# A decoder's per-head attentions on one core: an item's two value products side by side in TensorE's order

## The reference, cut to what matters

```python
# layer 0, self-attention: 16 heads of 16, LoRA projections
scores = einsum('bhqd,bhkd->bhqk', q, k) * SCALE
out = einsum('bhqk,bhkd->bhqd', softmax(scores), v)
# layer 1, self-attention: 16 heads of 16, causal, ALiBi bias
scores = where(causal, scores + bias, NEG)
# layer 1, cross-attention: 32 query heads of 8, 8 key heads
scores = einsum('bkgsd,bktd->bkgst', qh, kh) * scale
out = einsum('bkgst,bktd->bkgsd', softmax(scores), vh)
```

## Time and profile before

| | us |
|---|---|
| median of 3 runs (lowest, highest) | 950.26 (950.02, 950.55) |
| the profiled execution | 950.78 |
| its span in the trace | 948.6 |
| a0, first to last output copy | 63.21 to 118.57 |
| a1, last output copy | 676.35 |
| x1, first to last output copy | 735.67 to 830.39 |

### The profile page before, as it was taken

How to read it: one execution, slowest core, us unless ns; L and a number is a source line. 1 busy time by engine, 2 the same in 40 slices (tenths; PEclk the granted TensorE clock), 3 DMA queues, 4 the chain that set the end, 5 groups by cost and what they waited for, 6 DMA issues and landing times. The chain is left out here.

```text
span 948.6 us, 14084 instructions
## 1 busy us (share of the span) xinstructions
PE 762.5 (80%) x4818; PEld 483.7 (51%) x4818; DVE 592.4 (62%) x1129; ACT 422.8 (45%) x879; POOL 209.7 (22%) x313
## 2 busy tenths in 40 slices
PE   6888968899898998988362458889726999959998
PEld 3544655566666665665221233546512444348787
DVE  5557666564655656655765973456455999673765
ACT  4446732644535436345165334345332666612322
POOL 4312020303203023031303412221031212123441
PEclk9979989999999999999776557999955999987999
DMA  5957413110201201100210008693051111001311
GB/s 127 119 75 129 133 29 88 41 51 16 67 26 42 65 10 58 26 12 23 68 16 23 0 7 99 69 142 89 23 172 54 40 42 38 7 2 23 113 45 45
DMA packets 52356, 53.48 MB, mean 56 GB/s; under 512 B 11296, under 2 KB 41984, under 8 KB 52296
## 3 DMA queue, kind: packets, MB, share of 16 engines
q1 hardware_dynamic: 47772, 51.55, 26.1%
q10 hardware_dynamic: 4524, 1.14, 0.6%
HBM read 29.62 MB, written 5.09 MB: 37 GB/s over the span
## 5 line engine op out<-in xcount | busy, mean ns | idle before, releaser
L536 DVE TENSOR_REDUCE a_nm<-ps 128x2 f32<-128x512 f32 (+1 forms) x112 | 75.6, 688 | 52.0 <-PE ps L836 30.4
L1185 DVE TENSOR_REDUCE x_nm<-ps 128x2 f32<-128x512 f32 x128 | 84.9, 686 | 24.0 <-PE ps L1253 22.1
L679 ACT ACTIVATE a_pt<-ps 128x1024 f32<-128x1024 f32 x64 | 58.0, 916 | 49.1 <-PE ps L887 30.8
L1221 ACT ACTIVATE x_pt<-ps 128x1024 f32<-128x1024 f32 x64 | 62.1, 1021 | 33.1 <-PE ps L1290 33.1
L2007 PE MATMUL ps<-m_xp,m_mp 128*128 128x512 f32 x288 | 74.8, 400 | 1.9 <-DVE m_wr L1735 1.9
L1721 DVE TENSOR_TENSOR m_qcs<-ps,mw_tab 128x512 f32<-128x512 f32 x96 | 61.8, 686 | 22.0 <-PE ps L2007 21.1
L1884 ACT ACTIVATE m_junk<-ps,m_nm 128x256 bf16<-128x256 f32 x128 | 58.7, 486 | 37.0 <-DVE m_nm L1747 37.0
L1707 POOL TENSOR_SCALAR fw<-fw,finv 128x256 f32<-128x256 f32 x24 | 11.7, 486 | 254.8 <-PE ps L2087 254.8
L1253 PE MATMUL ps<-a_ks,a_qs 126*128 126x256 bf16 x256 | 53.3, 294 | 17.6 <-DMA a_ks<-scr_xk 16.1
L2007 PEld LDWEIGHTS ps<-m_xp,m_mp 128*128 128x128 f32 x288 | 52.2, 191 | 14.3 <-issue 4.9
L2816 PE MATMUL ps<-x_xp,x_wp 128*128 128x512 f32 x216 | 55.9, 410 | 0.3 <-DVE x_h3g L2738 0.3
(11 more groups left out here) (271 smaller groups left out, 1714.9 us busy)
## 6 DMA issues: line engine op xcount, KB each, us to landing
a_qs<-a_parts SPq DMA_DIRECT2D x48, 128.0 KB, 6.5
a_ks<-a_parts SPq DMA_DIRECT2D x48, 128.0 KB, 7.4
m_q<-m_qs SPq DMA_DIRECT2D x32, 128.0 KB, 2.2
x_gb<-scr_g SPq DMA_DIRECT2D x8, 512.0 KB, 3.6
fw<-in_f_w SPq DMA_DIRECT2D x12, 256.0 KB, 3.5
scr_xq<-xs_qp SPq DMA_DIRECT2D x12, 256.0 KB
a_qs<-scr_xq SPq DMA_DIRECT2D x32, 96.0 KB, 2.1
mw_wq<-in_m_wq SPq DMA_DIRECT2D x8, 256.0 KB, 2.9
```

Of the source, the lines that this page charges most:

```text
L536: dve.tensor_reduce(dst, src, AX.X, ALU.max, negate=True).then_inc(mx_done.sem, 1)
L679: act.activation(pt[:, n % 2, kt, 0:banks * BANK], c.ps[:, 2 + 2 * kt:2 + 2 * kt + banks, :].rearrange("p b n -> p (b n)"), ACT.Exp, scale ...
L1185: dve.tensor_reduce(dst, src, AX.X, ALU.max, negate=True).then_inc(mx_done.sem, 1)
L1221: act.activation(pt[:, i % 2, kt, 0:banks * BANK], c.ps[:, 2 + 2 * kt:2 + 2 * kt + banks, :].rearrange("p b n -> p (b n)"), ACT.Exp, scale ...
```

## The change

In the step of an item `product(n, 1)` moves up to stand directly behind `product(n, 0)`, ahead of `max_transpose` and of the third unit of scores. `scores_t(n + 1, 1)` moves from the end of the step to the place ahead of the fourth unit. The same edit is made in the loop of `attention_block` and in the body of `attention_stage`. In a1, which has no fourth unit, `scores_t(n + 1, 1)` stays the last of the step. The other engines' lists stay as they are.

```diff
                     scores_t(n + 1, 0)
                     scores(n + LAG, 1)
                     product(n, 0)
+                    product(n, 1)
                     max_transpose(n + TLAG)
                     scores(n + LAG, 2)
-                    product(n, 1)
+                    scores_t(n + 1, 1)
                     if UNITS == 4:
                         scores(n + LAG, 3)
-                    scores_t(n + 1, 1)
...
                         product(it, i, 0)
+                        product(it, i, 1)
                         ahead(max_transpose, it, i + TLAG, last)
                         ahead(scores, it, i + LAG, last, 2)
-                        product(it, i, 1)
+                        ahead(scores_t, it, i + 1, last, 1)
                         if UNITS == 4:
                             ahead(scores, it, i + LAG, last, 3)
-                        ahead(scores_t, it, i + 1, last, 1)
```

## The result

After the change the median is 953.84 us (6 runs, 952.49 to 955.53), the kernel before on the same chip 950.14 us (6 runs, 946.63 to 950.97): ratio 1.0048, 95% interval 1.0028 to 1.0067. The change costs +3.7 us where +8.1 was forecast: slower, as predicted, but by much less, and 0.2 us under 954, the low end of the range. The profiled execution took 954.16 us, its span is 952.0 (before 948.6).

The account below looks back on a forecast made before the run. Waits between TensorE and VectorE were taken to bound a0 and x1, TensorE alone a1. Terms x1 +6.9, a0 +2.5, a1 -1.3 sum to +8.1, giving 958.4 us; range 954 to 962.

Parts of the forecast that it names:

- TensorE's own order is the bound everywhere: Rival, all stages: TensorE's issue order sets every item, -0.2 us an item in x1 and a0, total 942.2; chance 0.09.
- S1 reuses the bank that R3 reads; the weight load ahead of S1 has 0.19 idle: x1 item: the second scores unit waits for the previous fourth reduce, 0.88 us from reduce start to scores.
- same loop; I take x1's +0.25: a0 stage: the same loop of waits as in x1 binds, so each item grows by 0.25 us.
- S0 waits for R2 as well: First scores unit also waits for the third reduce; that end plus 0.19 leads on no later than the fourth reduce.
- 6 x 0.25 = 1.5: a0 stage: six item intervals behind the transfer stall each grow by 0.25 us, +1.5 together.
- The term of x1, +6.9: x1 stage: 28 intervals times 0.24 us give 6.7, plus 0.2 at the end; bounds 5.9 and 7.5.
- the +0.2 for the last M: End of x1: the last `max_transpose` comes 0.46 us later behind the second product, half of it counted.
- the stall ends near 79.4: a0, item 6: the wait for its row of maxima, ending at 78.45 before, would end near 79.4.
- +1.0: a0 stall: SyncE's row of item 5 and the `send_high(3)` sends behind it come later, delaying item 6 by 1.0 us.
- The exponentials are not late: Rival, x1: the second product waits for a late exponential, overdrawn by 0.15 us an item, total 962.6; chance 0.06.
- the clock stays at 1.00: Rival: TensorE's idle of 0.45 us an item lowers its clock to 1.2 GHz; three such items give 966; chance 0.04.
- T1's 0.43 costs nothing now: x1 item before: the second `scores_t`, 0.43 us, lies under the fourth reduce, which holds back the second scores unit anyway.

Follow-up runs that it names:

- T1 back behind S3: The change, with the second `scores_t` again behind the fourth unit of scores in a0 and x1, against the kernel before: 952.87 us, ratio 1.0030.
- a0 alone: Only the a0 call of `attention_block` takes the new order, against the kernel before: 949.48 us, ratio 1.0001.
- x1 alone: Only the loop body of `attention_stage` takes the new order, against the kernel before: 953.84 us, ratio 1.0042.
- a1 alone: Only the a1 call of `attention_block` takes the new order, against the kernel before: 948.55 us, ratio 0.9987.

## Why the prediction was right and where it was wrong

**Right: TensorE's own time in the new order.** A0 to M was put at 0.92 and took 0.88; A0 to S2 at 1.07 and took 1.04 in x1 and 1.09 in a0. The Trainium skill (TensorEngine Tiling (Array Packing), Key Properties) says that changing the tiling mode drains TensorE. The runs show what the borders between products and other matmuls cost: an item of a1, which TensorE alone sets, is 0.24 shorter with two such borders fewer. That it is a drain no run shows by itself.

**Right that x1's loop binds, and by luck its length: the path is O's and not S1's.** From R3 to A0 the prediction counted 0.88 + 0.37 = 1.25 by way of S1, and it is 1.25 before (776.29 to 777.54) and after (778.31 to 779.56). But the path is R3, O, A0: 0.60 + 0.41 + 0.24; the way through S1 needs only about 1.07 (below). The two lengths agree because both were read off the same two events. The same chain closes to 3.18 before: 1.25 + 0.46 + 0.15 + 0.32 + 0.57 + 0.43. So in x1 VectorE's loop did bind ahead of the change, if barely: the items beside the loop's ends are 3.13 apart, where A0 follows S1 by 0.31 in TensorE's own order. From there on all that A1 adds ahead of S2 is paid. The rival "TensorE's own order is the bound everywhere" falls with that: x1 got 4.8 slower.

**The step that failed: "S1 reuses the bank that R3 reads; the weight load ahead of S1 has 0.19 idle", priced as R3 to S1 0.88 and carried to a0 ("same loop; I take x1's +0.25").** The idle was the weight load's at 777.03. The matmul S1 at 777.17 was due then anyway, by TensorE's own order: T0 at 776.74 and 0.43 more. 0.88 was the spacing of two events with slack between them, not the length of a dependency. After the change R3 ends at 778.99 and the matmul starts at 779.06, so R3 to S1 is at most 0.75, and 0.13 of the 0.88 was slack. In x1 this did no harm, since O's path makes up the 1.25. In a0 it did, since O's end leads to A0 sooner there. The timeline of a0 after:

```profile
93.08 1.07 PE L901 MATMUL ps<-a_pt,a_vs 128*32 128x256 f32 x16
...
94.18 0.39 PE L823 MATMUL ps<-a_ks,a_qs 96*128 96x256 bf16 x2
...
94.61 1.35 DVE L536 TENSOR_REDUCE a_nm<-ps 128x2 f32<-128x512 f32 x2 [0.46 <-PE ps L823]
...
95.87 0.41 DVE L544 TENSOR_SCALAR xnT<-ps 128x256 f32<-128x256 f32 x1
...
96.02 0.39 PE L823 MATMUL ps<-a_ks,a_qs 96*128 96x256 bf16 x2
...
96.34 0.85 PE L901 MATMUL ps<-a_pt,a_vs 128*32 128x256 f32 x12
```

O ends at 96.28 and A0 starts 0.06 later; R3 (95.28) to S1 is 0.74 and S1 to A0 0.32. By both ways R3 to A0 is about 1.06, not 1.25. With 1.10 to S2, 0.43 to R2 and 0.67 to R3 that makes 3.26. But a third way gives the same sum here: S0 waits for R2, and TensorE's own order leads on to S1 and A0. T1 back behind S3 tells them apart, since it brings R3 forward. The timeline of an a0 item of that kernel:

```profile
91.41 1.07 PE L901 MATMUL ps<-a_pt,a_vs 128*32 128x256 f32 x16
...
92.51 0.61 PE L823 MATMUL ps<-a_ks,a_qs 96*128 96x256 bf16 x4
...
92.94 1.29 DVE L536 TENSOR_REDUCE a_nm<-ps 128x2 f32<-128x512 f32 x2 [0.51 <-PE ps L823]
...
93.69 0.39 PE L823 MATMUL ps<-a_ks,a_qs 96*128 96x256 bf16 x2
...
94.14 0.41 DVE L544 TENSOR_SCALAR xnT<-ps 128x256 f32<-128x256 f32 x1
...
94.36 0.38 PE L823 MATMUL ps<-a_ks,a_qs 96*128 96x256 bf16 x2
```

R3 (0.61 after R2, at 93.55) ends 0.13 ahead of S1 (94.36), and O ends 0.12 ahead of the next A0 (94.67): neither is waited for, and still the item is 3.26. The loop is R2 to S0 0.75, S1 0.67, A0 0.31, S2 1.10, R2 0.43 = 3.26. With O moved away a0 has 3.26 as well. The prediction had this wait too ("S0 waits for R2 as well"), with the same 0.19 in it, and so with the same slack.

A0 and A1 of an a0 item before:

```profile
70.20 0.64 PE L901 MATMUL ps<-a_pt,a_vs 128*32 128x256 f32 x8
...
71.19 0.64 PE L901 MATMUL ps<-a_pt,a_vs 128*32 128x256 f32 x8
```

With A1 to S3 0.57 and S3 to R3 0.43 the loop through R3 was 1.06 + 0.99 + 0.57 + 0.43 = 3.05, 0.15 short of TensorE's own 3.20. The change used up that slack and 0.06 more. The term of a0's six items, "6 x 0.25 = 1.5", would be 6 x 0.06 = 0.4; a0 alone measures 0.6 (19.63 for the six intervals, before 19.05), since the last of them is 3.26 where it was 3.07.

**The term of x1, +6.9, was mis-sized: +4.8.** 0.04 of each item because A1 and M took 0.88 and not 0.92, and 0.02 because R2 to R3 is 0.66 and not 0.68: 3.38 in place of 3.43, where 3.41 was the forecast of 3.17 + 0.24. And not all items pay that: in the last body and beside the loop's ends they were 3.13 apart before and are 3.27 after, so +0.14. The output copies of x1 after (they answer to the earlier trace rows) give the sum:

```profile
735.20 0.41 DVE L1190 TENSOR_SCALAR x_av<-ps 128x256 f32 x1
...
825.53 0.41 DVE L1190 TENSOR_SCALAR x_av<-ps 128x256 f32<-128x256 f32 x1
```

90.33 for 27 intervals, before 85.52: +0.18 an item on average, 4.8. The last four copies take 9.18, before 9.20: the +0.2 for the last M is nothing.

**a1: right, and a little more than forecast.** The timeline of a1 after (it answers to the earlier trace rows), a product pair, M and S2:

```profile
654.75 0.86 PE L901 MATMUL ps<-a_pt,a_vs 128*32 128x256 f32 x16
...
655.42 0.28 PE L853 MATMUL ps<-identb,a_nms 128*8 128x128 bf16 x2
...
655.63 0.39 PE L831 MATMUL ps<-a_ks,a_qs 102*128 102x256 bf16 x2
```

A0 to M is 0.67, forecast 0.46 + 0.25 = 0.71. The item is 3.20, 0.24 under 3.44 and not 0.20. Over six intervals that is -1.4: from A0 of item 6 to A0 of item 12 it takes 18.50 after, and 19.85 with the old order in x1 alone and in a0 alone (before 20.56, with the slow clock in the first of them). The means of the stage differ by -1.6, the profiled pair by -2.1.

**a0's stall: "the stall ends near 79.4" came out, for no reason that the runs bear out.** The timeline of TensorE after (it answers to the earlier trace rows), and the window of the same item's clock:

```profile
79.42 0.61 PE L871 MATMUL ps<-a_qs,a_ks 98*128 98x256 bf16 x4 [1.50 <-DMA a_qs<-a_mT]
...
84.16 0.61 PE L871 MATMUL ps<-a_qs,a_ks 98*128 98x256 bf16 x4 [1.32 <-DMA a_qs<-a_mT]
...
85.10 1.93 PE L901 MATMUL ps<-a_pt,a_vs 128*32 128x256 f32 x16
...
89.75 0.63 PE L901 MATMUL ps<-a_pt,a_vs 128*32 128x256 f32 x6
```

```profile
85.20:86.20 1.00, 1.00 (x12) 0.49 (x16) 0.69 (x1) 0.69 (x1) 0.00 (x0) 0.50 1.25 146
```

79.42 is 0.97 later than before, but 0.73 of it was there ahead of the stage, and with the old order the stall ended at 78.45, 79.48 (x1 alone) and 79.71 (a1 alone), with the new one at 79.42 and 79.58 (a0 alone). In the run of x1 alone `send_high(3)` began at 69.75, before at 69.72 and after at 71.63: the sends are 1.9 later in the run after, and the row of maxima arrives no later than in an execution with the early sends. With the old order in a1 alone they began at 71.25. The time of the sends alone doesn't set the end of the stall, so the term "+1.0" has no support; what does set it is open. The granted clock falls to 0.50 (1.2 GHz) behind different idles: before it lay at 0.50 under the stall's own item, after it lay there in the next one, whose A0 to A0 is 4.65 (85.10 to 89.75) in place of 3.2. Split at A0 of item 6, the stage shows where the +1.1 of its means lies. From the first A0 up to there it takes 24.72, 25.74 and 24.97 with the old order and 24.76 and 25.25 with the new: no difference. The six intervals behind take 19.05, 19.05 and 19.06 with the old order, 19.63 in a0 alone and 21.02 after, where 1.4 is the one slow item. Whether the new order makes such an item likelier, two executions can't tell.

**The other signs.** VectorE idles ahead of R2 (0.51), not of R3: right. TensorE's weight load idles 0.41 ahead of S0 and 0.32 ahead of S1, released by the reduce: right as far as it goes, though its matmuls idle 0.30 an item and not 0.45, and in x1 part of that is ahead of A0. The exponentials are not late, and the clock stays at 1.00 in x1 at 0.3 us idle an item: those two rivals fall. "T1's 0.43 costs nothing now" was right too, and T1's new place costs 0.06 an item.

**The total.** x1 +4.8 for +6.9, a0 about +1.1 for +2.5, a1 -1.6 for -1.3: about +4.3 for +8.1. The greater part of the miss is x1's size (2.1), the next the a0 step (1.4), and 0.3 is a1's.

## What to carry to other kernels

The spacing of two events is a price only if the second one waits for the first; ahead of using it, work out when the second was due by its own engine's order, and look at the matmul's start rather than at its weight load's idle. Where two waits end together in one trace, only an experiment that moves one of them tells which binds: here T1's place did it. Where two loops of almost the same length run through a stage, write down both for each stage: a reordering that shortens TensorE's own sum pays off where TensorE alone sets the item (a1: -0.24) and is a loss where the result that it delays feeds VectorE back into the same loop (x1: +0.20). Moving the consumer to the other side of such a loop only swapped the wait here, since VectorE could take a product's result only 1.25 us after A0 began.

## What was unexpected of the hardware

- From O's end to A0's start it takes 0.24 us in x1 both before (777.30 to 777.54) and after, and 0.06 in a0. x1's waits are against values that a loop counts on and a0's are against constants; x1's last body, which has constants, is 0.05 an item shorter before (3.13, 3.18) and 0.11 after (3.27, 3.38). That the kind of the wait is the cause was not tried by itself, and it can't be all of it: the first two items of each round of x1's loop have 0.13 too (759.28 to 759.42 after). x1's A0 also has one wait more in the code than a0's (`v_in`), a rival that was not tried either.
- With O moved ahead of R2, VectorE starts on a product's result 1.25 us after A0's start in x1's loop, 0.8 after A1's, though A1's matmuls occupy TensorE for about 0.44. In a0 and in x1's last body it is 1.14.
- A small transpose between two products costs nothing in front (A0 to A1 0.46) and its time is paid behind (A0 to S2 1.09 on either side of A1).
- In the x1 loop R2 to R3 is 0.66 where S3 comes just in time and 0.61 where it lay ready.
